# Waits and load order where the scatters end and the experts begin, in a one-core decoder layer

## The reference, cut to what matters

```python
x = _layernorm(x + attn(x, w_q, w_k, w_v, w_o))
x = _layernorm(x + xattn(x, ctx_1024, w_sim, b_sim, W_qv, b_qv))
logits = x @ router_w.T + expert_bias
top_w, top_idx = jax.lax.top_k(sigmoid(logits), 8)
combine[t, top_idx] = 2.5 * top_w / sum(top_w)
routed = einsum('eti,ehi->th', silu(x @ w_gate[e].T) * combine.T[:, :, None], w_down)
shared = silu(x @ w_gate_shared.T) @ w_down_shared.T
x = _layernorm(x + routed + shared)
```

## Time and profile before

| | us |
|---|---|
| untraced, median of three runs | 903.72 (902.05 to 905.78) |
| traced execution, first to last instruction | 1049.1 |
| of it, `attend` | 0 to 290 |
| `mix` | 290 to 655 |
| `experts` | 655 to 990 |
| `combine` | 990 to 1049 |

### The profile page before, as it was taken

One profiled execution on the slowest core, in us unless ns is written; L12 is line 12 of the kernel. 1 busy time (PEld: TensorE's weight loads), 2 busy tenths in 40 slices (PEclk: granted clock), 3 DMA queues, 4 the chain that ended last, 5 costly groups with the idle time before them and its releaser, 6 DMA issues. The chain is left out here.

```text
span 1049.1 us, 14869 instructions
## 1 busy us (share of the span) xinstructions
PE 806.3 (77%) x3800; PEld 528.4 (50%) x3800; DVE 493.2 (47%) x1287; ACT 381.5 (36%) x809; POOL 356.9 (34%) x360
## 2 busy tenths in 40 slices
PE   8989999999868888297493210988888787898395
PEld 4644444444345656174262110766666665666274
DVE  1677777777142585256432941322222222322077
ACT  2247777767724334215111000233333333333101
POOL 9101011110000014635356470355555555555400
PEclk9989999999969989799597655888889998988799
DMA  6998777786511113311122135788888888886296
GB/s 229 316 334 267 262 258 270 274 278 232 186 45 44 37 52 107 118 65 74 58 78 98 55 110 180 244 272 273 262 268 266 278 267 249 269 266 204 91 422 254
DMA packets 103410, 207.45 MB, mean 198 GB/s; under 512 B 25863, under 2 KB 51505, under 8 KB 97088
## 3 DMA queue, kind: packets, MB, share of 16 engines
q1 hardware_dynamic: 64160, 128.94, 37.1%
q10 hardware_dynamic: 24320, 42.74, 12.4%
q0 software_dynamic: 14880, 35.17, 9.2%
HBM read 117.76 MB, written 96.08 MB: 204 GB/s over the span
## 5 line engine op out<-in xcount | busy, mean ns | idle before, releaser
L1738 POOL DMA_INDIRECT contributions<-c_c,e_dest x182 | 177.0, 973 | 183.2 <-ACT c_c L1719 123.4
L1886 POOL DMA_INDIRECT row_pool<-rows,places x128 | 127.1, 993 | 213.0 <-issue 155.3
L1693 DVE COPY e_xt<-e_psx 128x256 f32<-128x256 f32 (+1 forms) x130 | 67.5, 530 | 251.2 <-PE e_psx L1625 100.5
L541 DVE TENSOR_REDUCE a_mx<-a_psS 128x2 f32<-128x1024 f32 x128 | 152.0, 1218 | 30.8 <-PE a_psS L363 30.5
L1639 PE MATMUL e_psg<-e_xt,e_w 128*128 128x64 f32 (+2 forms) x676 | 134.9, 338 | 34.2 <-ACT e_g L1712 26.4
L499 ACT ACTIVATE a_e<-a_psT 128x512 f32<-128x512 f32 x256 | 135.5, 600 | 57.9 <-PE a_psT L393 51.6
L1639 PEld LDWEIGHTS e_psg<-e_xt,e_w 128*128 128x128 f32 x676 | 108.3, 218 | 45.1 <-issue 33.0
L1712 ACT ACTIVATE e_g<-e_psg 128x128 f32<-128x128 f32 (+1 forms) x130 | 42.2, 324 | 241.4 <-PE e_psg L1639 143.8
L1650 PE MATMUL e_psy<-e_w,e_g 128*128 128x256 f32 (+1 forms) x442 | 119.7, 435 | 10.8 <-ACT c_c L1719 6.2
L1719 ACT ACTIVATE c_c<-e_psy,e_weight 128x256 f32<-128x256 f32 x182 | 80.7, 475 | 72.9 <-PE e_psy L1650 30.3
L1625 PE MATMUL e_psx<-m_c,rows 128*128 128x128 f32 x364 | 69.9, 303 | 43.1 <-PEq L676 36.7
(11 more groups left out here) (284 smaller groups left out, 951.4 us busy)
## 6 DMA issues: line engine op xcount, KB each, us to landing
row_pool<-fill SPq DMA_DIRECT2D x32, 1260.0 KB, 7.2
e_w<-w ACTq DMA_DIRECT2D x156, 256.0 KB
rows<-row_pool SPq DMA_DIRECT2D x143, 140.0 KB
c_c<-contributions SPq DMA_DIRECT2D x16, 1024.0 KB, 17.3
a_k<-k_parts SPq DMA_DIRECT2D x64, 128.0 KB, 3.3
rows<-row_pool SPq DMA_DIRECT2D x78, 70.0 KB
a_q<-q_parts SPq DMA_DIRECT2D x32, 128.0 KB, 4.2
a_q<-q_parts SPq DMA_DIRECT2D x64, 64.0 KB, 3.4
```

What stands on the lines that cost most here:

```text
L541: nc.vector.tensor_reduce(mx[:, at.slot, qt, 2 * DH * pair::HALF], psS[:, pair], AX, ALU.max).then_inc(maxed, 1)
L1693: nc.vector.tensor_copy(XT[:, at.slot % XT_RING, 0:n], ps_x(at, 0, n)).then_inc(xt_done, 1)
L1738: nc.gpsimd.indirect_dma_start(out=contrib, out_offset=bass.IndirectOffsetOnAxis(ap=dest[:, result(f) + k:result(f) + k + 1], axis=0), in_ ...
L1886: nc.gpsimd.indirect_dma_start(out=pool, out_offset=bass.IndirectOffsetOnAxis(ap=place[:, b, t, k:k + 1], axis=0), in_=rows[:, b, t], in_o ...
```

## The change

The fourth scatter group of batches 0, 1 and 2 waits for `ranks_read` of the next batch in place of `um_done` and `routed`. In the last train POOL waits for `tables_spread` between the third and the fourth group. SP issues the weights of the first half, then the three waits and the row loads of the first half, then the weights of the second half.

```diff
-            for j in range(RING_E):
-                tables.load_weights(sp, w, j, first[HALF_OF[j]])
+            for j in ENTRIES_OF[0]:
+                tables.load_weights(sp, w, j, first[0])
 
             for r in range(2):
                 sp.wait_ge(sent[r], (B - r) // 2 * (16 * TT * TOP_K))
@@
             for j in ENTRIES_OF[0]:
                 tables.load_rows(sp, pool, j, first_pages)
+            for j in ENTRIES_OF[1]:
+                tables.load_weights(sp, w, j, first[1])
@@
                     dispatch(b, sent[b % 2], (2,))
-                    pool_eng.wait_ge(um_done, b + 3)
+                    pool_eng.wait_ge(ranks_read, b + 2)
                     dispatch(b, sent[b % 2], (3,))
                 else:
                     dispatch(b, sent[b % 2], (0,))
                     pool_eng.wait_ge(mixed, TT * B)
                     dispatch(b, sent[b % 2], (1, 2))
-                    pool_eng.wait_ge(routed, B)
+                    pool_eng.wait_ge(ranks_read, B)
                     dispatch(b, sent[b % 2], (3,))
             pool_eng.wait_ge(rows_done, B)
             pool_eng.sem_inc(dispatching, 1)
-            dispatch(B - 1, last_sent, range(TT))
+            dispatch(B - 1, last_sent, range(TT - 1))
+            pool_eng.wait_ge(tables_spread, 1)
+            dispatch(B - 1, last_sent, (TT - 1,))
```

## The result

The changed kernel takes **907.51 us** (median of 20 executions, 904.80 to 910.80) beside 905.78 us for the kernel before (20, 902.05 to 907.07) on the same chip. The ratio is 1.0026, with a 95% interval of 1.0015 to 1.0037: 1.4 to 3.4 us slower, by the ratio 2.4 us (the two medians lie 1.7 us apart, inside this interval). Measured once more on another occasion (the last experiment) it was 1.0027 [1.0012, 1.0042]. The prediction was 906.2 us, a cost of 2.5 us on a base of 903.72 us (the median of the first three of the 20 executions of before), and "the same" by the bound of 0.5%.

A forecast was written before the change was run, and what follows sets the result against it. `mix`, where the change lies, was taken as a chain of small steps bound by who waits for whom. Fourth group 0, pause 0 and weights in two parts +2.5 us on a median of 903.7 gave 906.2 us, range 902 to 909.

The forecast's parts named there:

- The late releases: In `mix`, VectorE's semaphores move late while POOL scatters; nearly none assumed in timed runs, at most 0.49 of 69.9 us.
- the 145 us: Whole kernel: traced span 1049.1 us against median 903.72; 145.4 us must be missing somewhere, at least 36 from `mix`.
- the seven rows: VectorE's long waits in the second half of `mix`, nearly all ending in "remote", together 69.9 us.
- The rival of partly real releases: In `mix`, part of the late semaphore releases also occurs in timed runs; a quarter gives 10 us, 893.7 us; chance 0.20.
- The fourth group: POOL's wait for `ranks_read` in three batches of `mix`: even if it binds, POOL is free 0.5 us early; 0 us.
- The pause: POOL's last train: spread lists released 2.9 us before the 24th scatter ends, so the wait costs 0 us.
- The split: SP at the end of `mix`: six weights behind the row loads delay the exit; +2.5 us, bounds 0 and +3.3.
- L - S: End of `mix`: time from release of the spread lists (S) to landing of the last scattered rows (L), 14.6 us.
- Every later load follows from TensorE's start: In `experts`, after the later start nothing is gained back, as all later loads follow TensorE's start; no size given.
- Late rows: Start of `experts`: TensorE's start hangs on row loads, so moving six weights behind them frees 5.2 us; 898.5 us, chance 0.08.
- VectorE blocked by the moved group: `grow`, `put`, `places` of steps 2 to 4: scalar and copy operations wait for scatters, 8.7 us; 912.4 us, chance 0.12.

The follow-up runs named there:

- the repeat: The kernel before, unchanged, run and traced again: 905.04 us, traced span 902.6 us.
- the kernel with all weights behind: Against the kernel before, SP issues all thirteen first weights behind the row loads: 910.95 us, ratio 1.0063.
- the one-entry kernel: Against the kernel before, SP issues only the first entry's two row loads in `mix`, the other seven at the start of `experts`: 904.68 us, ratio 0.9994.
- the split alone: Against the kernel before, only the first weights issued in two parts around the row loads: 906.87 us, ratio 1.0012.
- the pause alone: Against the kernel before, only POOL's wait for the spread lists before the last train's fourth group: 905.20 us, ratio 0.9997.
- the extra products: Against the kernel before, 17 unused TensorE products between the landing of the last scatters and the exit of `mix`: 905.05 us, ratio 1.0002.
- ScalarE's weights: Against the kernel before, ScalarE issues the second half's six weights in `mix` after the scatters landed, beside SP's row loads: 903.80 us, ratio 0.9981; again 903.37, 0.9983.
- the group-only experiment: Against the kernel before, only the fourth groups' waits changed to `ranks_read`: 906.73 us, ratio 1.0004.

## Why the prediction was right, and where its steps were not

**The late releases.** Right in the conclusion, that a timed run has none of them, which kept some 40 us of apparent gain out of the forecast. The reason given (the 145 us must be missing somewhere) was sound, but it left up to 0.49 of them possible; the repeat shows none. Its sum was not clean: the last of the seven rows, 6.1 us, ends in "issue" and is no late release (63.8 us are left, and the bound is 0.44), and `combine` was left out as a place where time could be missing. By the repeat `experts` gave 81.7 us, `mix` 61.9, `attend` and `combine` 1.3 and 1.5. The forecast that the traced span would fall by some 40 us was wrong: it fell by 146.5 us, since the whole execution shown had been slower, `experts` too. The rival of partly real releases (893.7 us) has nothing left.

**The fourth group, 0 us**: right, and more simply than argued. The bound that was worked out for a wait that binds (eight scatters in 11.0 us) was not needed, because POOL comes to the group after the ranks are read.

**The pause, 0 us**: right, for the reason given: the lists are released before POOL's 24th scatter ends. They come at 564.83 us, the 24th ends at 569.07, 4.2 us later where 2.9 was forecast.

**The split, +2.5 us**: right as to the place and the sign. The exit of `mix` releases TensorE, and the six weights stand in front of the exit: 3.03 us where 3.3 was forecast. **The step that failed is the term L - S = 14.6 us**, the landing of the last scatters after the lists. It was read where no weight load was in flight while POOL scattered, because there the lists came only after POOL's end. In an undisturbed execution the weight loads run beside the scatters, and L - S is 18.6 us before (584.12 - 565.48) and 16.8 us in the changed kernel (581.64 - 564.83). Two things follow that the sum did not have. The thirteen issues never covered the landing, which comes 4.0 us after their end, so all six moved issues count. And the split itself makes the landing 1.8 us earlier. With the measured terms: -1.7 us until the row loads begin (17.6 in place of 19.3 us after the lists), +3.0 us for the six weights, together +1.3 us at TensorE's first row, and 1.3 us by the table.

The time says +2.4 us (1.4 to 3.4). Of the rest, the trace has 1.1 us between TensorE's first row and the first reload, where the clock rises later. Put together these make 2.35 us, and the repeat of the changed kernel shows the same 2.4 us at its first reload. That agrees with the time, and so do the kernel with all weights behind (+5.6 us at the first reload, +5.7 timed) and the one-entry kernel (-0.3 and -0.5). For the clock also speaks that the timed executions of the changed kernel and of the split alone have the lower granted clock; those of the pause alone have not, so that the reload 2.1 us late in its one trace tells little of its time. **It is not shown to be the cause**: the extra products had the reload 1.2 us early and gained nothing, and in the first trace of the changed kernel `experts` from TensorE's first row on are as long as before (253.29 and 253.26 us) in spite of the later reload. So the cost of the split at TensorE's start is shown; the second half of the 2.4 us stays open between the clock and the spread of what follows. That 2.5 was forecast and 2.4 measured is in part luck: the forecast's terms came out 1.2 us too high, and about as much was added that it did not have.

**"Every later load follows from TensorE's start"** was too strong. A later start went with a longer time (all weights behind: 4.4 us later, 5.7 timed); an earlier one, of 3.6 or 6.2 us, was given back within the measurement's 1 to 1.5 us, since the rows bind next.

**The rivals.** Late rows (898.5 us): the rows did move 1.7 us forward, but the exit behind them moved back, and TensorE is released by the exit in both. VectorE blocked by the moved group (912.4 us): the group was not moved, as POOL had never waited there, and `mix` up to the last train takes 248.87 us against 249.41. So this rival was not put to the test by the change. What stood beside the scatters before stands there still: in the fourth group of batch 0 a scalar operation of `places` (L1231, L1235 in the changed kernel) takes 0.37 us in both kernels, and 0.18 in the earlier trace rows.

ScalarE's weights are the version that beats both, at 0.9981 and 0.9983 of before. Half of its reason held (TensorE starts 1.1 us earlier), but its gain shows in `mix` before the edited place, 248.0 us against 249.4, in both of its traces. There TensorE's clock stays at the upper level where it falls before, and twelve products take 1.7 us less. That this is the timed gain too is not shown: the timed executions' mean clock is 0.9238 and 0.9240, that of before 0.9231 and 0.9237.

## What to carry to other kernels

Before a load is moved behind a wait, ask what it delays from where it stands now: loads in flight beside scatters make the scatters land later, so part of the issue time that the move costs comes back in the wait. An engine's release by a block's exit shows what its start hangs on, not that an earlier start is worth anything: look at what binds the second instruction. And where a traced span and the timed median differ by 145 us, trace again before reasoning from its waits.

## What the runs showed of the hardware

The landing of a POOL scatter depends on what SP has in flight. The last record came 1.2 us after POOL's end with no weight loads ahead, 1.8 to 2.7 us with seven of 256 KB and 4.1 to 4.6 us with thirteen; in the repeat of before the DMA engines' share was 1.03 to 1.06 meanwhile. The Trainium skill, DMA: Bandwidth & Descriptors, section Queues, rings and completion order, says that each DMA engine takes turns between the queues that have work for it, packet by packet; the rows fit that, as the scatters get through beside the loads, but later.

POOL's scatters took 1.29 to 1.42 us instead of 0.97 beside some of VectorE's work in the fourth group (the rows of the group-only experiment), while VectorE's operations on two inputs there (L1206 to L1216 of the changed kernel) took 0.82 us, as in the same lines before the first scatter. Of its scalar operations most kept their time beside scatters; single ones took 0.32 us instead of 0.24 (L1191, beside the third group) and 0.37 instead of 0.18 (L1235). The Trainium skill, SBUF — State Buffer, section Who interferes with whom, says that a VectorE instruction with two inputs in SBUF contends with a GpSimd instruction that reads SBUF; that fits in kind, but which instruction met which was not tried.

After the same first rows of work TensorE's granted clock rose to the upper level some 2.2 us later in both traces of the changed kernel than in the repeat of before. TensorE had been idle for 27.7 and 26.4 us before its first row, and its instructions are the same. In the trace of the pause alone, with SP's order as before, it rose 6.5 us after the first row. Why the one rise comes so much later was not found.
